# A value block's way through DRAM is cut in halves, and two steps of the last sequence change places

## The reference

```python
gate_v = jnp.einsum('btc,hec->bthe', x, Ws)
w, sel = jax.lax.top_k(gate_v, K)                          # K = 2 of E = 8
wsig = jax.nn.sigmoid(w)
oh = jax.nn.one_hot(sel, E, dtype=x.dtype)
mix_v = jnp.einsum('bthk,bthke->bthe', wsig, oh)
proj_v = jnp.einsum('btc,edc->bted', x, Wv)
v = jnp.einsum('bthe,bted->bhtd', mix_v, proj_v)           # the mixed values
scores = jnp.einsum('bhid,bhjd->bhij', q * scale, k)
attn = jnp.einsum('bhij,bhjd->bihd', jax.nn.softmax(scores, axis=-1), v)
gate_o = jnp.einsum('btc,hec->bthe', x, Wd)
_, sel_o = jax.lax.top_k(gate_o, K)
mask_o = jax.nn.one_hot(sel_o, E, dtype=x.dtype).sum(axis=3)
res = jnp.einsum('bthe,bthd,efd->bthf', mask_o, attn, Wo)
return res.sum(axis=2)
```

## Time and profile before

| | value |
|---|---|
| three runs, median (lowest to highest) | 1359.17 us (1358.05 to 1361.2) |
| profiled execution, its own time | 1362.38 us |
| its span, first to last instruction | 1360.7 us |
| TensorE busy, matmuls | 1150.3 us, 85% of the span |
| TensorE's mean granted clock | 0.808 of full speed |
| VectorE, ScalarE, GpSimd busy | 697.2, 495.0, 77.5 us |
| DMA, mean over the span | 42 GB/s |

### The profile page before, as it was taken

How to read it: one execution, slowest core, us unless ns; L and a number is a source line. 1 busy time by engine, 2 the same in 40 slices (tenths; PEclk the granted TensorE clock), 3 DMA queues, 4 the chain that set the end, 5 groups by cost and what they waited for, 6 DMA issues and landing times.

```text
span 1360.7 us, 21174 instructions
## 1 busy us (share of the span) xinstructions
PE 1150.3 (85%) x8499; PEld 893.7 (66%) x8499; DVE 697.2 (51%) x1867; ACT 495.0 (36%) x1022; POOL 77.5 (6%) x134
## 2 busy tenths in 40 slices
PE   6879788998889888998889888998889988996566
PEld 4548555886569755886569755886569755785466
DVE  5513685347743676347743676347753676334500
ACT  4234333541534433441524433451524433432200
POOL 0010001000010001000000001000000001000000
PEclk8658876897879986898869976898869976898655
DMA  7000010302103120302103130302103030303122
GB/s 206 0 0 4 1 31 15 70 17 51 42 9 66 43 56 15 70 16 52 40 10 66 35 64 14 71 16 52 39 11 66 32 66 13 66 18 82 42 51 51
DMA packets 197520, 56.84 MB, mean 42 GB/s; under 512 B 173056, under 2 KB 193326, under 8 KB 197422
## 3 DMA queue, kind: packets, MB, share of 16 engines
q1 hardware_dynamic: 195118, 51.20, 17.7%
q10 hardware_dynamic: 2304, 4.29, 1.0%
HBM read 31.36 MB, written 24.12 MB: 41 GB/s over the span
## 4 chain that ended last, share of the span: by engine, by line
PE 72%; DVE 13%; ACT 7%; issue 4%; SPq 2%; DMA 1%; ACTq 0%; DVEq 0%
PE bank L891 10%; PE bank L712 9%; PE bank L748 9%; PE bank L638 7%; DVE negmax L1224 4%; PE bank L853 4%; PE bank L818 4%; PE bank L599 3%; ACT pa L985 3%; PE bank L653 3%; PE bank L874 3%; PE bank L563 2%; PE bank L832 2%; PE bank L905 2%; PE bank L663 2%
## 5 line engine op out<-in xcount | busy, mean ns | idle before, releaser
L985 ACT ACTIVATE pa<-bank 128x512 f32<-128x512 f32 x224 | 123.5, 596 | 119.7 <-PE bank L638 52.5
L1224 DVE TENSOR_REDUCE negmax<-bank 128x2 f32<-128x512 f32 (+1 forms) x224 | 139.0, 683 | 33.0 <-PE bank L501 17.5
L891 PE MATMUL bank<-vb,pb 128*128 128x65 f32 x1024 | 133.1, 293 | 12.9 <-issue 12.9
L891 PEld LDWEIGHTS bank<-vb,pb 128*128 128x128 f32 x1024 | 129.6, 209 | 17.7 <-issue 16.0
L1002 ACT ACTIVATE pa<-bank,b_c 128x256 f32<-128x256 f32 x256 | 107.5, 471 | 91.2 <-PE bank L712 89.9
L712 PE MATMUL bank<-xnT_a,w 128*128 128x256 f32 x512 | 137.2, 416 | 0.1
L748 PE MATMUL bank<-w,pa 128*128 128x128 f32 x1024 | 125.4, 276 | 0.0
L748 PEld LDWEIGHTS bank<-w,pa 128*128 128x128 f32 x1024 | 122.4, 192 | 3.2
L1309 DVE SCALAR_TENSOR_TENSOR x_a<-bank,wr,x_a 128x128 f32<-128x128 f32 x128 | 38.8, 344 | 149.8 <-PE bank L748 149.5
L712 PEld LDWEIGHTS bank<-xnT_a,w 128*128 128x128 f32 x512 | 101.2, 208 | 17.0 <-issue 3.5
L638 PE MATMUL bank<-pa,va 128*32 128x256 f32 (+1 forms) x1024 | 96.2, 526 | 17.1 <-ACT pa L985 14.5
(11 more groups left out here) (240 smaller groups left out, 1737.4 us busy)
## 6 DMA issues: line engine op xcount, KB each, us to landing
v_d<-vb SPq DMA_DIRECT2D x16, 512.0 KB, 4.9
vb<-v_d SPq DMA_DIRECT2D x16, 512.0 KB, 5.9
at_d<-at SPq DMA_DIRECT2D x32, 256.0 KB, 2.1
at<-at_d SPq DMA_DIRECT2D x32, 256.0 KB, 4.3
pv_d<-pvs SPq DMA_DIRECT2D x8, 512.0 KB, 2.8
pvs<-pv_d SPq DMA_DIRECT2D x16, 256.0 KB, 4.5
w<-in_L_ffn_W_dram ACTq DMA_DIRECT2D x1, 2048.0 KB, 10.6
bd<-mix_d SPq DMA_DIRECT2D x128, 8.0 KB
```

Of the source, the lines that this page charges most:

```text
L891: mm = pe.matmul(BB[2 + qt][:, i * (DH + 1):(i + 1) * (DH + 1)], pb[:, h % NPB, kt * T + qt * P:kt * T + (qt + 1) * P], vb[:, kt, h, :], s ...
L985: nc.scalar.activation(pa[:, e % NPA, :], BA[e % 2][:, :], ACT.Exp, scale=SC0).then_inc(S["a_ex"], 1)
L1224: nc.vector.tensor_reduce(negmax[:, i:i + ng], BA[j][:, :].rearrange("p (g k) -> p g k", g=ng), AX, ALU.max, negate=True).then_inc(S["a_mx ...
```

## The change

It does five things.

1. ScalarE evicts the mixed values into at, no longer into vb.
2. SyncE writes each half to v_d behind its own eviction, so that four DMAs of 8 groups take the place of two of 16 groups. It reads back in halves too: two DMAs fill partitions 0 to 63 of vb once the first half's writes have landed, and two fill partitions 64 to 127 once the second half's have.
3. The eight DMAs that fill bd from sel_d are a step of their own, b_sel, and stand behind the reads. The first fill of bd, from mix_d, becomes the step b_fill at its old place.
4. TensorE's b_mix also waits until the maxima have been taken and cT has been copied (b_mx, b_cc), by rules that would allow b_mix among the maxima. With the order used here all eight b_max stand ahead.
5. The last sequence has a list of its own, with the same steps as the others, but all at position 68 of A (56*7+68 = 460).

```diff
+        LAST_B = list(STEPS_B)
+        LAST_AFTER = [68] * len(LAST_B)
+
+        def stream_b(q):
+            return (LAST_B, LAST_AFTER) if q == B - 1 else (STEPS_B, AFTER_A)
...
+                for k, (name, i) in enumerate(stream_b(q)[0]):
+                    timed.append((q * len(STEPS_A) + stream_b(q)[1][k], k + 1, name, i, q))
...
                     def b_mix(half):
-                        if half != 1:
-                            return
-                        for t in range(NT):
-                            sp.wait_ge(S["b_ve"], upto("b_ve", 3 + t))
-                            sp.dma_start(v_d[t].rearrange("g s h d -> (s h) g d"), vb[:, t, :, 0:DH]).then_inc(S["b_vd"], 16)
+                        groups = slice(8 * half, 8 * half + 8)
+                        for t in range(NT):
+                            sp.wait_ge(S["b_ve"], upto("b_ve", NT * half + t + 1))
+                            sp.dma_start(v_d[t, groups].rearrange("g s h d -> (s h) g d"), at[:, t, groups, :])\
+                                .then_inc(S["b_vd1" if half else "b_vd0"], 16)
+                        if half == 1:
+                            for part in range(2):
+                                sp.wait_ge(S["b_vd1" if part else "b_vd0"], upto("b_vd0", 16 * NT))
+                                for t in range(NT):
+                                    sp.dma_start(vb[64 * part:64 * part + 64, t, :, 0:DH],
+                                                 v_d[t, 8 * part:8 * part + 8].rearrange("g s h d -> (g s) h d"))\
+                                        .then_inc(S["b_vr"], 16)
+
+                    def b_sel(_):
                         sp.wait_ge(S["b_bz"], upto("b_bz", 2))
                         for i in range(T8):
                             sp.dma_start(bd_o[HB * i:HB * i + HB, :, i, :],
                                          sel_d[:, i].rearrange("n h e -> h n e")).then_inc(S["b_do"], 16)
-                        sp.wait_ge(S["b_vd"], upto("b_vd", 32))
-                        for t in range(NT):
-                            sp.dma_start(vb[:, t, :, 0:DH], v_d[t].rearrange("g s h d -> (g s) h d")).then_inc(S["b_vr"], 16)
...
                         if half == 0:
                             pe.wait_ge(S["b_dm"], upto("b_dm", 16 * NT * T8))
                             pe.wait_ge(S["b_pr"], upto("b_pr", 16 * NT))
-                            pe.wait_ge(S["b_cc"], upto("b_cc", 1))
                         else:
                             pe.wait_ge(S["b_ve"], upto("b_ve", NT))
+                        done = maxima_before(now[0], half)
+                        if done > 0:
+                            pe.wait_ge(S["b_mx"], upto("b_mx", 2 * done))
+                        else:
+                            pe.wait_ge(S["b_lo"], upto("b_lo", 8))
+                        if done == 8:
+                            pe.wait_ge(S["b_cc"], upto("b_cc", 1))
...
                         if hg == 0:
-                            pe.wait_ge(S["b_vr"], upto("b_vr", 16 * NT))
+                            pe.wait_ge(S["b_vr"], upto("b_vr", 32 * NT))
...
-                            nc.scalar.copy(vb[:, t, 8 * half:8 * half + 8, 0:DH],
+                            nc.scalar.copy(at[:, t, 8 * half:8 * half + 8, :],
                                            BB[2 + t][:, :].rearrange("p (g d) -> p g d", d=DH)).then_inc(S["b_ve"], 1)
```

More of the change, by code:

```diff
@@ L219, in transformer_program @@
             b_mx=16, b_ct=1, b_cc=1, b_st=16, b_ex=16, b_mw=1, b_pd=16, b_pr=32, b_bz=2, b_md=32, b_dm=256, b_do=128,
-            b_mm=4, b_ve=4, b_vd=32, b_vr=32, b_pv=8, b_at=8, b_ad=64, b_ar0=32, b_ar1=32, b_z=2, b_zc=2, b_ro=2, b_xo=2,
+            b_mm=4, b_ve=4, b_vd0=32, b_vd1=32, b_vr=64, b_pv=8, b_at=8, b_ad=64, b_ar0=32, b_ar1=32, b_z=2, b_zc=2, b_ro=2, b_xo=2,
             a_out=16)
@@ L361, in transformer_program @@
         STEPS_B = [("b_norm", 0), ("b_norm_apply", 0), ("b_gates", 0), ("b_split", 0), ("b_top2", 0),
-                   *run("b_split", 1, 5), ("b_top2", 1), *run("b_split", 5, 8), ("b_top2", 2), *run("b_max", 0, 8),
-                   ("b_shift", 0), ("b_score", 0), ("b_mix", 0), ("b_score", 1), ("b_mix", 1),
+                   *run("b_split", 1, 5), ("b_top2", 1), *run("b_split", 5, 8), ("b_top2", 2), *run("b_max", 0, 4), ("b_fill", 0), *run("b_max", 4, 8),
+                   ("b_shift", 0), ("b_score", 0), ("b_mix", 0), ("b_score", 1), ("b_mix", 1), ("b_sel", 0),
                    ("b_score", 2), ("b_score", 3), ("b_attend", 0), ("b_score", 4), ("b_score", 5),
@@ L366, in transformer_program, with maxima_before @@
                    ("b_weigh", 0), ("b_gather", 0), ("b_gather", 1), ("b_out", 0)]
-        AFTER_A = (60, 62, 63, 64, 65, 65, 65, 67, 67, 67, 67, 69, 71, 72, 72, 72, 75, 76, 76, 77, 80, 81, 82, 82,
-                   85, 86, 86, 86, 90, 98, 99, 105, 105, 106, 112, 113, 114, 114, 117, 117, 117)
+        AFTER_A = (60, 62, 63, 64, 65, 65, 65, 67, 67, 67, 67, 69, 71, 72, 72, 72, 75, 76, 76, 76, 77, 80, 81, 82, 82, 85, 86, 86, 86, 86, 90, 98, 99, 105, 105, 106, 112, 113, 114, 114, 117, 117, 117)
         assert len(AFTER_A) == len(STEPS_B)
+        LAST_B = list(STEPS_B)
+        LAST_AFTER = [68] * len(LAST_B)
+        def stream_b(q):
+            return (LAST_B, LAST_AFTER) if q == B - 1 else (STEPS_B, AFTER_A)
+        def maxima_before(q, half):
+            steps = stream_b(q)[0]
+            place = steps.index(("b_mix", half))
+            count = sum(name == "b_max" for name, _ in steps[:place])
+            assert count < 8 or steps.index(("b_shift", 0)) < place
+            return count
         def merged():
@@ L438, in b_top2, with b_fill @@
                                      top_b[0][:, :].rearrange("p (k t n) -> p k t n", k=2, t=NT)[:, 1]).then_inc(S["b_md"], 16)
-                    def b_max(m):
-                        if m != 3:
-                            return
+                    def b_fill(_):
                         sp.wait_ge(S["b_md"], upto("b_md", 32))
@@ L482, in b_out @@
                             sp.wait_ge(S["a_out"], upto("a_out", 16))
-                    own = dict(f_load=f_load, s_first=s_first, b_gates=b_gates, b_split=b_split, b_top2=b_top2, b_max=b_max, b_mix=b_mix,
+                    own = dict(f_load=f_load, s_first=s_first, b_gates=b_gates, b_split=b_split, b_top2=b_top2, b_fill=b_fill, b_mix=b_mix, b_sel=b_sel,
                                b_attend=b_attend, b_weigh=b_weigh, b_out=b_out)
@@ L828, in b_max @@
                             pe.wait_ge(S["b_mx"], upto("b_mx", 2 * m - 2))
+                        for half in range(2):
+                            if m - 1 <= maxima_before(now[0], half) <= m:
+                                pe.wait_ge(S["b_ve"], upto("b_ve", NT * half + NT))
                         for c in range(2):
@@ L839, in b_shift @@
                         pe.wait_ge(S["b_mx"], upto("b_mx", 16))
+                        for half in range(2):
+                            if 6 <= maxima_before(now[0], half) < 8:
+                                pe.wait_ge(S["b_ve"], upto("b_ve", NT * half + NT))
                         turn_tokens(BB[2], negc, S["b_ct"])
```

3 lines of the change are left out of this document (removed).

## The result

The changed kernel took 1364.22 us in the median of 20 runs (1360.47 to 1368.22), the kernel before 1360.13 us in 20 runs beside them (1356.63 to 1364.43). The ratio is 1.003, with a 95% interval of 1.0018 to 1.0041: slower by some 4 us, outside the range that was forecast. Their spans are equal (1360.3 and 1360.7 us), so the two profiles have to be compared stretch by stretch. They differ before the change's place already: b_out's additions of sequence 6 start at 1240.44 us here and at 1243.83 before, and over all the profiles of this study at 1239.2 to 1245.7 us. The scatter between executions is as large as the effect.

What follows compares the result with a forecast made beforehand. It took TensorE's matmuls, busy 1150.3 of 1360.7 us, as the bound, with waits in the last sequence to change. Terms -6.4 + 2.5 + 2.0 = -1.9 us gave a median of 1357.3 us, eight-in-ten range 1353.0 to 1361.5.

Steps and rivals of the forecast that it cites:

- Where the cost sits: All sequences: nothing expected from seven of the eight; the price of the change is set in the last one.
- The norm behind b_out: Last sequence's b_norm, queued behind b_out's additions on VectorE: its time stands open, 2.5 us more.
- Reads that come sooner: Reads of vb ahead of the last sequence's attended products: the first product starts at 1296.1, not 1302.50, 6.4 us less.
- The clock behind the gap: Last sequence's transposes, gates and value projections: TensorE's 3.6 us idle gap drops them to 1.2 GHz, 2.0 us more.
- The sum: Whole kernel: the three terms together give -1.9 us, for an expected median of 1357.3 us.
- Rival (b): Last sequence's reads come no sooner to any use: 1.5 us gained against 4.5 lost, +3.0, 1362.2 us; chance 0.09.
- Rival (c): Last sequence's attended products run at full clock after the shorter wait: 13.1 us saved, 1344.2 us; chance 0.03.

Runs made afterwards that it cites:

- e1: Changed kernel with the last sequence's steps back at their old places, b_norm ahead of b_out again; 1358.51 us, ratio 0.9974 to the kernel before.
- e2: Kernel before with only the last sequence's steps all moved to position 68; ratio 1.0054 to the kernel before.
- e6: Changed kernel with three spare matmuls into an unused bank ahead of TensorE's wait for xn_b in the last sequence; ratio 1.0003 to the kernel before.
- e9: e5 with whole reads of vb (two DMAs, 128 partitions), issued once both halves of the writes have landed; ratio 0.9948 to the kernel before.
- e5: e1 with the eight fills of bd (b_sel) moved behind b_attend 0 in every sequence; ratio 0.9982 to the kernel before.
- e8: e7 plus a 256-column spare matmul ahead of the wait in six later b_max and eight ahead of the last b_gather; ratio 0.985 to the kernel before.
- e7: e5 with eight spare matmuls ahead of the last sequence's first attended product; 1341.1 us, ratio 0.9852 to the kernel before.
- e11: Kernel before with only thirteen spare matmuls added ahead of the last sequence's first attended product; ratio 0.9915, five runs at 1339.69 to 1343.05 us, seven at 1354.43 to 1361.31.
- e10: e7 with eight more spare matmuls ahead of the last b_gather, none among the maxima; 1335.43 us, ratio 0.9805 to the kernel before.

## Why the prediction was wrong

**Where the cost sits: right.** The last sequence holds the whole effect, the earlier ones nothing (e1, e2, and the even distances of pv_d's writes).

**The norm behind b_out, +2.5 us: right.** 2.56 in after and in e2, 2.55 in e6.

**Reads that come sooner, -6.4 us: mis-sized.** 3.85 us (before to e1), or 4.17 (e2 to after). The failed step is "The second part also queues behind the first part's 512 KB, which flow from 1290.4 to 1292.8": I let reads into half of the partitions run at the writes' rate. They run at some 155 to 165 GB/s, over 6 us for 1 MB, where I had 4.8. Counted from the second half's copies, the last data came after some 9.7 us in the changed kernel and the first product after 11.0, where I had 7.8 and 8.7. e9, whose reads reach all partitions, ran at 212 to 274. "so the packets of 256 B limit it at about the same rate" was wrong with it: the packets are the same in e5 and e9. The Trainium skill (SBUF — State Buffer, Door 1: The DMA port swizzle) says that half the partitions reach half the ports, which I priced at 0.3 to 0.6 us. The runs agree with it in direction, at 1.8 us instead (6.3 against 4.5), though they don't separate the partitions from the DMAs' number and size. It gives 196 GB/s for 1 MiB, and the rate measured here, with DMAs of 256 KB, is below it. The row that I leaned on, pvs<-pv_d, has one DMA in each half of the partitions, so its shape was the same and its target was not. It was short as well, 512 KB, and its rate fell inside the pair. In e5 the first of 1 MB also ran fast, at 272 GB/s from 1291.5 to 1292, and most of it at about 155. Windows of pvs<-pv_d before, then of e5:

```profile
1253.80:1254.20 0.40, 0.00 (x0) 0.00 (x0) 0.40 (x1) 0.00 (x0) 0.00 (x0) 1.00 1.16 265
...
1255.40:1255.80 0.40, 0.00 (x0) 0.00 (x0) 0.40 (x2) 0.00 (x0) 0.00 (x0) 1.00 1.38 190
```

```profile
1291.50:1292.00 0.50, 0.00 (x0) 0.00 (x0) 0.00 (x0) 0.10 (x1) 0.00 (x0) 1.00 1.21 272
```

How much of the pair's higher rate is its target and how much its shortness isn't shown.

**The clock behind the gap, +2.0 us: mis-sized, and its reach wrong.** Gates and values lost 2.89 us, more than my "all low". The sentence that failed is "Behind the projections VectorE's selection chain is late, not TensorE, and hides the low clock." That holds up to b_shift (27.2 us in every profile but e8's), but in the mixing products after it the level rose within 10 us with the norm early (before, e1) and not before the wait for vb with the norm late (after, e2). That is another 1.1 us (e1 to after) to 1.4 (before to e2). The term had nothing for it. By what route a gap some 40 us earlier does this stays open, as the level was back at 1.00 in between.

**The sum.** -3.85 + 2.56 + 2.89 + 1.07 = +2.7 us, where I had -1.9; with 0.35 behind the first product, the stretch shows 3.02. The runs say 4.1 (0.18 to 0.41%). Rival (b), slower at +3.0 through late reads, had the right sign, and its +3.0 beside the stretch's 3.02 is luck. It put the reads' gain at 1.5 us, where 3.85 came, and laid the loss to the fills, which took 0.9 us of it (e1 to e5), the rate of the half reads the larger part; the rest of the slowdown was the clock's. It had 0.09, which was too little: three unsure terms of 2 to 6 us had been summed as if only the first could go wrong.

**Rival (c), the full clock in the last products,** I gave 0.03 for this change, rightly, since the shorter wait still drops the level. Its price for the 128 products, put at 13.1 us, was 13.2 in e7, and 16.6 with the scores between them.

What stays open: why e9 was timed 4 us below e5, why the level doesn't rise in the mixing products with the norm late, and what gives the second sequence its two lengths, 5 to 6 us apart, which is most of the scatter between profiles of one kernel's code.

## What to carry to other kernels

Compare the sorted order of all steps before and after a change, not only the steps that it names: a list of positions for the last iteration alone moved one vector norm behind a matrix step, and that cost more than the change's purpose gained. Where the last iteration runs with nothing beside it, look at TensorE's clock behind each wait before looking at the wait: here the work behind such a wait took 16.6 us more at the low level than at the full one (e5 and e7), and matmuls into an unused bank that ended 1.1 to 1.3 us ahead of the data gave that back. Ended 1.95 us ahead, they didn't in the execution that was profiled. Compare a DMA with one that has the same target partitions and as much data behind it, not only the same shape. And before reading a difference of 4 us out of two profiles, compare the stretches that the change can't touch: here one of them differed by 6 us.

## What the runs showed of the hardware

- Reads of 256 B packets from DRAM ran at 154 to 166 GB/s into 64 partitions at a time (e5, four DMAs of 256 KB, behind a start at up to 272), with the DMA share at 1.4, and at 212 to 274 into 128 (e9, two DMAs of 512 KB).
- The attended products kept a granted clock of 1.00 when they came behind busy matmuls (e7), with the scores between them did not raise one of 0.50 in 38 us (before, after), and let it fall behind an idle wait of 1.95 us (e11, the one profiled execution); behind waits of 1.10 and 1.29 us it held (e7, e10).
- In profiles with the same code up to there, the second sequence ran with the granted clock at 0.50 or at 1.00 from 212 to 224 us, and was 155.8 or 149.6 us long (e1, after).
